# Reordering one step of a hand-written plan in the last stage of a four-stage model kernel

## The reference, cut to what matters

```
o_flat = normalised(o) * gn_weight + gn_bias
o_flat = o_flat + bonus
x = x + (o_flat * g) @ W_o
...
tokens = layer_norm(x)
logits = tokens @ gate_weight.T
top1 = argmax(logits);  rank = running count of each expert's tokens
x = x + residual + weight * expert_out[top1, rank]
```

## Time and profile before

| what | us |
|---|---|
| median of 3 timed runs | 4454.21 (4453.38 to 4456.28) |
| profiled execution, its own time | 4475.04 |
| its span, first to last instruction | 4473.3 |
| mean granted TensorE clock, as a share of full speed | 0.932 |
| the block `finish_and_route` in the span | about 3933 to 4219 |

### The profile page before, as it was taken

The page is one execution under the profiler, slowest core; times in us unless marked ns, Lnnn a source line. Parts: engine busy times, 40 slices in busy tenths (PEclk is TensorE's granted clock), DMA queues, the critical chain, the costliest instruction groups (busy, mean ns, idle before and its releaser), DMA issues. The chain is left out here.

```text
span 4473.3 us, 72079 instructions
## 1 busy us (share of the span) xinstructions
PE 3935.0 (88%) x23448; PEld 2685.1 (60%) x23448; DVE 3218.0 (72%) x8707; ACT 2194.9 (49%) x7361; POOL 2060.3 (46%) x1668
## 2 busy tenths in 40 slices
PE   5999999999996696988849999999999999936598
PEld 2344444444435464666638888888888888835466
DVE  5777777877745111789869999999999999946310
ACT  2666666666665211444404565555655555613211
POOL 2211211211223421111248888888888888725422
PEclk7999999999996798999979999999999999967699
DMA  4322332332346232244342323232322223166232
GB/s 111 82 74 70 100 79 70 87 88 63 79 96 214 74 128 84 104 169 169 150 102 31 42 34 43 34 42 34 41 35 39 37 36 41 15 181 219 80 127 80
DMA packets 479034, 378.41 MB, mean 85 GB/s; under 512 B 298378, under 2 KB 440997, under 8 KB 472544
## 3 DMA queue, kind: packets, MB, share of 16 engines
q1 hardware_dynamic: 466400, 348.90, 32.0%
q0 software_dynamic: 12288, 25.28, 1.7%
HBM read 222.13 MB, written 159.58 MB: 85 GB/s over the span
## 5 line engine op out<-in xcount | busy, mean ns | idle before, releaser
L750 DVE TENSOR_REDUCE at_neg_max<-at_slot 128x1 f32<-128x512 f32 (+3 forms) x1216 | 745.8, 655 | 247.5 <-PE at_slot L542 244.4
L672 ACT ACTIVATE at_prob<-at_slot 128x512 f32<-128x512 f32 (+1 forms) x1216 | 632.4, 579 | 354.3 <-PE at_slot L562 353.4
L2157 PE MATMUL sc_added<-sc_outer,sc_ident 128*128 128x128 f32 x4096 | 585.5, 286 | 78.8 <-POOL sc_outer L1908 58.0
L2157 PEld LDWEIGHTS sc_added<-sc_outer,sc_ident 128*128 128x128 f32 x4096 | 496.4, 191 | 209.3 <-DVE sc_state L2058 115.0
L1921 POOL TENSOR_TENSOR sc_terms<-sc_seen,sc_pack 128x1024 f32<-128x1024 f32 (+2 forms) x288 | 604.7, 2151 | 13.7 <-PE sc_ps_o L2179 13.7
L2179 PE MATMUL sc_ps_o<-sc_terms,sc_ident 128*128 128x256 f32 x2048 | 607.0, 381 | 2.1 <-POOL sc_terms L1921 2.1
L390 POOL TENSOR_SCALAR_AFFINE_SELECT at_prob<-at_prob 128x512 f32<-128x512 f32 x256 | 162.9, 636 | 888.2 <-ACT at_prob L672 888.0
L2081 ACT ACTIVATE sc_seen<-sc_state 128x512 f32<-128x512 f32 x256 | 153.1, 598 | 749.1 <-DVE sc_decayed L2022 740.2
L542 PE MATMUL at_slot<-at_k_stack,at_q_stack 96*128 96x512 bf16 (+3 forms) x1536 | 459.4, 335 | 22.0 <-DMA at_k_stack<-parts 19.5
L1908 POOL TENSOR_TENSOR sc_outer<-sc_pack 128x2048 f32<-128x2048 f32 x128 | 467.3, 3672 | 5.0
L562 PE MATMUL at_slot<-at_q_stack,at_k_stack 99*128 99x512 bf16 (+3 forms) x1536 | 452.7, 331 | 12.2 <-ACT at_prob L672 11.8
(11 more groups left out here) (306 smaller groups left out, 7155.8 us busy)
## 6 DMA issues: line engine op xcount, KB each, us to landing
packed<-pr_pack SPq DMA_DIRECT2D x16, 3072.0 KB, 13.4
sc_pack<-packed SPq DMA_DIRECT2D x512, 96.0 KB, 3.6
parts<-at_parts SPq DMA_DIRECT2D x96, 256.0 KB
f_up_w<-in_ffn_wi SPq DMA_DIRECT2D x16, 1024.0 KB
f_down_w<-in_ffn_wo SPq DMA_DIRECT2D x16, 1024.0 KB
at_q_stack<-parts SPq DMA_DIRECT2D x32, 384.0 KB
at_k_stack<-parts SPq DMA_DIRECT2D x32, 384.0 KB
slots<-at_no_row SPq DMA_DIRECT2D x2, 4128.0 KB
```

The source lines that it names most:

```text
L672: act.activation(prob[:, first:first + n, q1 - tiles * P:q1], ps[:, 0:n * tiles * P].rearrange("p (n k) -> p n k", n=n), ACT.Exp)\
L750: dve.tensor_reduce(neg_max[:, chunk, qt, h:h + n], ps[:, 0:n * tiles * P].rearrange("p (n k) -> p n k", n=n), AX.X, ALU.max, negate=True) ...
L2157: pe.matmul(added[h][:, 0:HALF], ident[:], outer[m % 2][:, 2 * n + s, h * HALF:(h + 1) * HALF], start=(s == 0), stop=False)
```

## The change

One step of the list is put in another order. No stage is added or dropped, and the entries that stand ahead of the loop stay. `place` keeps its batch (b - 2), `weigh_o` and `bias` theirs (b + 1).

```
     plan = of("bias", 0) + of("weigh_o", 0)
     for b in range(BATCH + 2):
-        plan += of("weigh", b - 2) + of("bias", b + 1) + parts("y_turn", b) + parts("r_turn", b - 1) + of("count", b - 2)
-        plan += parts("y_out", b) + of("gate", b - 1) + of("stats", b) + of("place", b - 2)
-        plan += of("weigh_o", b + 1) + of("affine", b) + of("choose", b - 1)
+        plan += of("bias", b + 1) + of("weigh_o", b + 1) + of("weigh", b - 2) + parts("y_turn", b) + parts("r_turn", b - 1)
+        plan += of("count", b - 2) + parts("y_out", b) + of("gate", b - 1) + of("place", b - 2) + of("stats", b)
+        plan += of("affine", b) + of("choose", b - 1)
     return plan
```

## The result

The changed kernel takes 4428.95 us (median, 4428.28 to 4430.12), the kernel before, timed beside it, 4454.85: ratio 0.9943, 95% interval 0.9931 to 0.9955. Predicted were 4425 us, with a range of 4413 to 4438, and a ratio of 0.9935. In the profile the span is 4427.2 us.

The account below looks back on a forecast made before the run. A chain of waits through weigh_o bounded the block; after the change GpSimd's scatters and bias would pace four steps. Gains of 5.4 + 10.6 + 4.2 + 8.9 = 29.1 us take 4454.2 to 4425, range 4413 to 4438.

Parts of the forecast that it names:

- GpSimd's chain: Middle steps: place, eight scatters, bias, weigh_o's last two passes and adds set 25.7 us in four steps, not 21.2.
- The square root: On VectorE after stats: it loses its cover and costs a wait of 0.4 us, bounds 0.3 and 1.7.
- rival 1: Middle steps: GpSimd doesn't set the pace, all steps take 21.2 us, 18 more gained, 4407 us; 5%.
- rival 2: Middle steps: no scatter is held by weigh_o's first pass, 24.8 us a step, 4421 us; 10%.
- rival 4: Middle steps: GpSimd's chain comes out at 27.6 us a step, so the middle gains nothing, 4433 us; 10%.
- rival 6: Middle steps: scatters are held by all VectorE work above them, 33.9 us a step, 4466 us; 5%.
- rival 5: Loads ahead of weigh_o set the pace and give back the 29 us, about 4454, no change; 5%.
- The first steps: From the block's start to batch 2's reciprocal: gains of 5.4, another 10.6 and another 4.2 us.
- The step without weigh_o: Step 7, where no scatter stands ahead of a bias: 21.2 us by VectorE's chain.
- The tail: After the last reciprocal (tok, choose, gate, last scatters): unchanged; 5.1 us more won if the 5.76 us wait goes.
- rival 3: Tail: VectorE's 5.76 us wait before L1477 goes away with the new timing, 4420 us; 17%.
- The middle: Reciprocal of batch 2 to that of batch 7: 124.0 us instead of 132.9, a gain of 8.9.

Follow-up runs that it names:

- Runs 2 and 6: 2: weigh_o and bias moved, place still behind stats, against the kernel before, 4442.99 us; 6: changed kernel plus four extra GpSimd passes of bias's size, ratio 0.9972.
- second profile: The kernel before, unedited, profiled again after the change was measured: 4453.44 us, its last-stage block 280.4 us.
- first profile: The profiled execution of the kernel before from which the prediction was read: 4475.0 us, against a timed median of 4454.9.
- run 3: Only place moved ahead of stats, weigh_o left between stats and affine, against the kernel before: 4467.68 us against 4456.83, ratio 1.0026.
- run 4: The changed kernel with GpSimd's bias of batch b + 2 ahead of the scatters of b - 2: 4425.29 us, ratio to the kernel before 0.9926.
- run 5: The kernel before with one extra unused GpSimd pass of bias's size ahead of bias for batches 4 to 7: ratio 1.0003.

## Why the prediction was right

The mechanism was right (weigh_o leaves the loop, and GpSimd's chain becomes the bound), and the gain was 3 us off (29 predicted, 25.9 timed). That it came so near is in part luck: two pairs of errors cancelled, as shown below. By points, from the block's start, the reciprocals of batches 0, 1, 2 and 7 were to stand at 47.5, 66.0, 89.4 and 213.5 us; they stand at 48.6, 67.6, 91.5 and 215.4.

- **What moves.** TensorE, ScalarE, GpSimd and SyncE kept their order; only VectorE's changed. weigh_o left the loop: the waits before the adds are gone in the middle steps.
- **The square root.** A wait of 0.28 to 0.35 us, 0.4 predicted.
- **GpSimd's chain.** 25.7 us predicted for four steps, measured 25.36, 25.23, 25.23 and 25.65. The eighth scatter is held (2.41, predicted 2.6), the seventh is not; L1400 waits 5.49 (predicted 18.35 - 12.96 = 5.4). The adds and their hop take 2.4 instead of 2.8, which is most of what is missing from 25.7. Runs 2 and 6 show that it is this chain, so rival 1 is out; the held eighth scatter puts out rival 2, the steps of 25.2 to 25.7 rival 4, and the 0.98 of the others rival 6. L1398 waits for loads in no middle step: rival 5 is out.
- **A sum that is right by luck.** From reciprocal 2 to 7 it is 123.9, predicted 124.0. The four steps were put 1.3 us too long in all, and the one behind them 1.2 too short.
- **The first steps were put too fast, by 1.1 us to R(0) and by 0.5 to 0.6 in each of the next two.** What was missing from the first: I gave a hold by GpSimd's bias only to the passes of weigh_o, and none to small operations of VectorE. In the changed kernel two of these are held, one by bias of batch 2 and one by bias of batch 3:

```profile
3966.60 2.16 DVE L1420 TENSOR_SCALAR f_roots<-f_mean_var 128x8 f32<-128x8 f32 x1
...
3992.95 4.12 DVE L1462 CAST f_earlier_bf<-f_earlier 128x8 bf16<-128x8 f32 x1
```

  They take 0.17 us otherwise, and both end within 0.04 us of bias. The first makes R(0) 2.0 us late, partly made good since the loads landed 0.7 earlier. The second stands in the place of the hold that I had given to L1398 of batch 3, so it cost little more than that. The 0.6 us between R(0) and R(1) are no hold: the stretch from reciprocal to last add took 14.2 instead of 13.6, the term of the next point.
- **The step without weigh_o** took 22.4, 21.2 predicted. I carried the 15.1 us from reciprocal to last add over as if it were fixed. It grew to 16.4, and y_out starts 8.8 us after the reciprocal instead of 8.0. TensorE had idled 5.7 us before r_turn instead of running y_turn just ahead of it. Its granted clock from the reciprocal to y_out is 0.50 of full speed (1.2 GHz, the lower of its two levels) instead of 0.71 in the same stretch of the step of the earlier trace rows, and the second half of r_turn takes 1.97 us instead of 1.15. No run changed the clock by itself, so that it is the cause rests on these rows. That stretch and the next in the changed kernel, by windows (columns as in the earlier trace rows):

```profile
4113.55:4122.30 8.75, 3.98 (x23) 3.55 (x24) 4.95 (x21) 8.16 (x16) 5.51 (x7) 0.50 0.43 140
4122.38:4129.90 7.52, 7.52 (x40) 6.64 (x37) 2.07 (x3) 2.53 (x4) 0.00 (x0) 0.95 0.01 3
```

- **The tail.** Predicted unchanged, with rival 3 at 17% (the 5.76 us go). In the second profile they are not there before the change either, so no gain came from that. Nor would it have been 5.1 us: the tail of that profile is 40.8 us, only 2.4 shorter than the first one's 43.2, since GpSimd's scatters are late next. But in the changed kernel the tail is 38.0 us from the last reciprocal, against those 40.8: GpSimd's groups of scatters were back to back there, and the first of the three now starts 3.2 us before the reciprocal instead of 1.0 after it. I had ruled this out because scatter 6 waits for place(6); in the second profile it waited for GpSimd.

Against the second profile of before, the 27.0 us are 3.3 to R(0), 9.9 and 3.7 in the next two steps, 7.3 in the middle and 2.8 in the tail. Predicted were 5.4, 10.6, 4.2, 8.9 and 0. The middle is smaller since 1.6 us of the 8.9 were one long step (4043.38 to 4072.57) of the first profile. Up to R(7) the prediction is 4.8 us too high, 2.8 of it because the first profile made before look that much longer than the second does, and 2.0 by its own terms. The 2.8 of the tail, which it had ruled out, made up for more than half of that: this is the second piece of luck.

Of the two rules of the Trainium skill (SBUF — State Buffer, "Who interferes with whom"), the first was that tensor_tensor was not seen to stall descriptor generation on GpSimd. It does hold scatters here, 2.41 us against 0.98, so the measurement goes against the page. The second, that a tensor_scalar in a two-port mode and GpSimd lock each other out, I set aside by the scatters beneath affine. They are indeed not held (0.98 to 1.05). But against bias the rule describes what is seen: L1437 7.77 us, L1420 2.16, a cast 4.12. The loss of run 3 fits it.

## What to carry to other kernels

When a stage leaves one engine's loop, walk the queue of the engine that feeds it: the next bound is often there, and its period can be added up from the same rows as the old one. Moving two stages together can be worth much more than each alone (place alone lost 11 us, with weigh_o moved it was worth 14), since what counts is on what the other engine's long pass falls. If the profiled execution is longer than the timed ones, or has a wait without an explained cause, profile the kernel before again, and on more than one chip: a wait can come back on some chips and be absent on others.

## What the runs showed of the hardware

- GpSimd's tensor_tensor of 128 x 2048 holds VectorE's tensor_scalar and cast from SBUF until it ends, small ones too: a cast of 128 x 8 took 4.12 us instead of 0.17, a tensor_scalar of 128 x 8 2.16. It holds a small tensor_tensor with two SBUF sources as well (L1453 in run 4, 128 x 64: 4.10 instead of 0.23).
- Other operations beneath it are not held: batch statistics (2.71 us for eight, as without it), adds with a source in PSUM (0.69), a tensor_reduce (L1456, 0.22), a memset (L1460, 0.07), and a reciprocal. In run 5 a reciprocal and a tensor_scalar follow each other on VectorE, both beneath the same bias, the third row:

```profile
4004.90 0.24 DVE L1432 RECIPROCAL f_scale<-f_std 128x16 f32<-128x16 f32 x1
4005.18 4.21 DVE L1433 TENSOR_SCALAR f_base_scale<-f_scale 128x8 f32<-128x8 f32 x1
```

```profile
4003.70 5.66 POOL L1275 TENSOR_TENSOR f_bonus<-f_bonus,f_wide_b 128x2048 f32<-128x2048 f32 x1 [25.48 <-DMA f_og<-gate]
```

  In these rows the kind of operation decides, and not its size or when it comes.
- Scatters from GpSimd (indirect DMA) are held by VectorE's tensor_tensor with two SBUF sources: 1.9 to 2.4 us instead of 0.98 in the kernels before and after, the eighth scatter until about 0.86 after the pass. They are not held by tensor_scalar (0.98 to 1.05 beneath L1437), and a pass of VectorE that starts while a scatter runs is not lengthened (2.28).
